# Adding the window mask on VectorE instead of on TensorE in six layers of local attention

## The reference

```python
mask = (it < jb) | (it > jb + w) | (jb == -1)
sim = jnp.einsum('bhwie,bhwje->bhwij', bq, bk2) * QK_SCALE
sim = jnp.where(mask, -jnp.finfo(sim.dtype).max, sim)
attn = jax.nn.softmax(sim, -1)
...
for i in range(DEPTH):
    x = attn_layer(shift_tokens(x), Wqkv[i], q_scale[i], k_scale[i], Wo[i]) + x
    x = ffn_layer(shift_tokens(x), ln_g[i], ln_b[i], W1[i], b1[i], W2[i], b2[i]) + x
```

## Time and profile before

| what | value |
|---|---|
| time, median of 3 runs | 3788.91 us (3785.52 to 3793.87) |
| time of the profiled execution | 3794.89 us |
| its span on the core | 3793.1 us |
| mean granted TensorE clock over the span | 0.936 |
| TensorE matmul busy | 3143.8 us (83%) |
| VectorE busy | 2479.8 us (65%) |
| ScalarE busy | 2071.4 us (55%) |
| GpSimd busy | 2292.4 us (60%) |

### The profile page before, as it was taken

The page is one execution under the profiler, slowest core; times in us unless marked ns, Lnnn a source line. Parts: engine busy times, 40 slices in busy tenths (PEclk is TensorE's granted clock), DMA queues, the critical chain, the costliest instruction groups (busy, mean ns, idle before and its releaser), DMA issues. The chain is left out here.

```text
span 3793.1 us, 121537 instructions
## 1 busy us (share of the span) xinstructions
PE 3143.8 (83%) x52983; PEld 2305.8 (61%) x52983; DVE 2479.8 (65%) x3404; ACT 2071.4 (55%) x2481; POOL 2292.4 (60%) x1606
## 2 busy tenths in 40 slices
PE   3169899899899998858888888888888888888885
PEld 2146677677677776636666666666666666666664
DVE  5456667677667776346676666766766766667664
ACT  2125555555555554426666666666666666666663
POOL 1334444444444543057777787777777777777773
PEclk7579999999999999979999999999999999999997
DMA  4344444445444444042222222322232222222221
GB/s 106 56 68 78 78 77 80 77 78 84 74 79 83 73 86 75 10 134 60 54 53 75 73 54 61 85 57 58 52 92 56 53 72 75 53 62 52 54 61 37
DMA packets 277483, 260.21 MB, mean 69 GB/s; under 512 B 106264, under 2 KB 220841, under 8 KB 276825
## 3 DMA queue, kind: packets, MB, share of 16 engines
q1 hardware_dynamic: 276232, 252.24, 31.3%
q10 hardware_dynamic: 720, 0.20, 0.0%
HBM read 98.30 MB, written 40.37 MB: 37 GB/s over the span
## 5 line engine op out<-in xcount | busy, mean ns | idle before, releaser
L659 ACT ACTIVATE prob<-psS 128x1024 f32<-128x1024 f32 x512 | 524.6, 1025 | 666.2 <-PE psS L536 664.5
L810 DVE TENSOR_TENSOR colmax<-psS,colmax 128x1024 f32<-128x1024 f32 x480 | 584.2, 1217 | 447.4 <-PE psS L536 447.2
L536 PE MATMUL psS<-diag,pst 128*128 128x64 bf16 x16384 | 596.2, 196 | 9.3 <-issue 9.3
L528 PE MATMUL psS<-qst,kst 48*128 48x128 bf16 (+1 forms) x8192 | 382.4, 224 | 257.6 <-DMA pst<-p_parts 187.1
L536 PEld LDWEIGHTS psS<-diag,pst 128*128 128x128 f16 x16384 | 530.3, 100 | 72.5 <-issue 21.2
L1263 PE MATMUL R<-wqkv,xsT 128*128 128x512 f32 x1152 | 557.5, 607 | 1.5 <-ACT qT L1399 1.1
L528 PEld LDWEIGHTS psS<-qst,kst 48*128 48x128 bf16 (+1 forms) x8192 | 241.6, 97 | 408.3 <-issue 157.3
L1527 POOL TENSOR_TENSOR pr<-pr,rnq 128x1024 f32<-128x1024 f32 x96 | 182.8, 1905 | 392.9 <-DVE pr L1608 392.9
L508 POOL TENSOR_TENSOR rel<-f,top 128x1024 f32<-128x1024 f32 x61 | 144.5, 2368 | 428.5 <-DVE top L815 428.0
L570 PE MATMUL psO<-prob,v 128*9 128x128 f32 x8192 | 329.3, 278 | 12.4 <-issue 11.8
L744 POOL TENSOR_TENSOR rel<-rel,rec 128x1024 f32<-128x1024 f32 x64 | 151.0, 2360 | 259.3 <-DVE rec L823 259.3
(11 more groups left out here) (190 smaller groups left out, 6274.5 us busy)
## 6 DMA issues: line engine op xcount, KB each, us to landing
v<-vs SPq DMA_DIRECT2D x576, 128.0 KB, 2.4
pst<-p_parts SPq DMA_DIRECT2D x512, 128.0 KB, 5.0
p_parts<-stage SPq DMA_DIRECT2D x64, 512.0 KB, 3.1
v<-vs SPq DMA_DIRECT2D x384, 64.0 KB, 2.0
wqkv<-in_L_ffn_Wqkv SPq DMA_DIRECT2D x18, 512.0 KB
q_stack<-qpart SPq DMA_DIRECT2D x6, 512.0 KB
qst<-q_stack SPq DMA_DIRECT2D x32, 96.0 KB, 6.0
wo<-in_L_ffn_Wo SPq DMA_DIRECT2D x6, 512.0 KB
```

The lines of the kernel that those rows point to most:

```text
L528: pe.matmul(dst[:, hp, P * p:P * (p + 1)], kst[r, pair, P * jb:P * (jb + 1)], qst[r, par, pair, :], start=(p == 0), stop=False, skip_group ...
L536: last = pe.matmul(o, pst[:, par, g, P * jb:P * (jb + 1)], diag[:, par, g, h0:h0 + HH // 2, :], start=False, stop=(g == NG - 1), skip_grou ...
L659: act.activation(prob[:, st % 2, :], psS[:, slot_of("b", st)].rearrange("p a b -> p (a b)"), ACT.Exp)\
L810: dve.tensor_tensor(dst, src, dst, ALU.max).then_inc(a_read, 1)
```

## The change

The mask is no longer put into R[3] by TensorE ahead of the scores. The score products open the accumulation themselves, and VectorE adds the float32 mask while it moves the scores from PSUM to `pr` in SBUF. The maximum and the subtraction then read `pr`. The output projection, which reuses R[3], waits for that addition (`masked_done`) and no longer for the subtraction. The bf16 copies of the mask and the identity, made once at the start, go away.

```diff
--- before.py
+++ after.py
@@ -1081,9 +1081,7 @@
         xm = sb("xm", [P, NB + 1, D])
         rope = sb("rope", [P, NB, 4 * LD])
         mask32 = sb("mask32", [P, 2, 2 * WIN])
-        mask = sb("mask", [P, NB, 2 * WIN], BF16)
         ident = sb("ident2", [P, P])
-        identb = sb("identb", [P, P], BF16)
         xs_a = sb("xs_a", [P, 2, D])
         xs_f = sb("xs_f", [P, D])
         xsT = sb("xsT", [P, 2, P])
@@ -1127,7 +1125,7 @@
 
         names = """init_dma init_dve init_pool w_dma xs_f_dma xT_done xT_ready q_done k_done v_done sq_done
             tq_done tk_done ssq_done clamp_done rn_done add_done kn_done qT_done kT_done qT_ready kT_ready
-            s_done mx_done sub_done scaled_done exp_done sum_done rden_done pT_done pT_ready pv2_done o_ready
+            s_done masked_done mx_done sub_done scaled_done exp_done sum_done rden_done pT_done pT_ready pv2_done o_ready
             oT_done oT_ready wo_done x2_done st_done lnv_done eps_done rstd_done xn_done xnT_done xnT_ready h_done
             hb_done gelu_done g_done gT_done gT_ready w2_done xmb_done x3_done v_ready tab_done prev_done q_added out_dma
             pool_taken dve_taken sp_taken""".split()
@@ -1216,9 +1214,6 @@
                 dve.memset(xm[:, 0, :], 0.0)
                 dve.memset(has_prev[:, 0:1], 0.0)
                 dve.memset(has_prev[:, 1:NB], 1.0)
-                dve.tensor_copy(identb[:], ident[:])
-                dve.tensor_copy(mask[:, 0, :], mask32[:, 0, :])
-                dve.tensor_copy(mask[:, 1:NB, :], mask32[:, 1:2, :].broadcast_to([P, NB - 1, 2 * WIN]))
                 dve.wait_ge(m["init_pool"], 6)
                 dve.tensor_tensor(xa[:, 1:NB + 1, :], xm[:, 1:NB + 1, :], mv16[:, :, 0:1].broadcast_to([P, NB, D]),
                                   ALU.subtract).then_inc(m["init_dve"], 1)
@@ -1343,16 +1338,12 @@
                         wait(pe, m["qT_ready"], n + 1)
                         wait(pe, m["kT_ready"], n + 1)
                         wait(pe, m["o_ready"], n)
-                        mk = slot(mask, n % NB)
-                        for half in range(2):
-                            pe.matmul(R[3][:, half, :], identb[:], mk.unsqueeze(1).broadcast_to([P, PAIRS, 2 * WIN]),
-                                      start=True, stop=False, skip_group_check=True)
                         for i in range(PAIRS):
                             for w in range(NW):
                                 last = pe.matmul(flat[3][WIN * w:WIN * (w + 1), P * i:P * (i + 1)],
                                                  qT[:, 1 - par, i, WIN * w:WIN * (w + 1)],
                                                  kT[:, 1 - par, i, :, WIN * w:WIN * (w + 2)],
-                                                 start=False, stop=True, skip_group_check=True)
+                                                 start=True, stop=True, skip_group_check=True)
                         last.then_inc(m["s_done"], 1)
                     if a:
 
@@ -1384,7 +1375,7 @@
 
                         wait(pe, m["oT_ready"], u + 1)
                         if b:
-                            wait(pe, m["sub_done"], n + 1)
+                            wait(pe, m["masked_done"], n + 1)
                         w = slot(wo, wp(u))
                         for i in range(PAIRS):
                             last = pe.matmul(flat[3][:, 0:D], otT[:, i, :], w[:, D * i:D * (i + 1)],
@@ -1601,13 +1592,15 @@
                         dve.tensor_tensor(gs[:], hs[:, 0, :], hs[:, 1, :], ALU.mult).then_inc(m["g_done"], 1)
                     if b:
                         wait(dve, m["s_done"], n + 1)
-                        dve.tensor_reduce(mx[:], flat[3].rearrange("p (h k) -> p h k", k=2 * WIN), AX.X, ALU.max)\
-                           .then_inc(m["mx_done"], 1)
+                        wait(dve, m["pT_done"], n)
+                        heads = pr[:].rearrange("p i a k -> p (i a) k")
+                        allowed = mask32[:, 0 if n % NB == 0 else 1, :].unsqueeze(1).broadcast_to([P, LH, 2 * WIN])
+                        dve.tensor_tensor(heads, flat[3].rearrange("p (h k) -> p h k", k=2 * WIN), allowed, ALU.add)\
+                           .then_inc(m["masked_done"], 1)
+                        wait(dve, m["masked_done"], n + 1)
+                        dve.tensor_reduce(mx[:], heads, AX.X, ALU.max).then_inc(m["mx_done"], 1)
                         wait(dve, m["mx_done"], n + 1)
-                        wait(dve, m["pT_done"], n)
-                        dve.tensor_tensor(pr[:].rearrange("p i a k -> p (i a) k"),
-                                          flat[3].rearrange("p (h k) -> p h k", k=2 * WIN),
-                                          mx[:].unsqueeze(2).broadcast_to([P, LH, 2 * WIN]), ALU.subtract)\
+                        dve.tensor_tensor(heads, heads, mx[:].unsqueeze(2).broadcast_to([P, LH, 2 * WIN]), ALU.subtract)\
                            .then_inc(m["sub_done"], 1)
                     if a:
                         rotate(s, par, 1, 1, "tk_done")
```

## The result

| | before | after |
|---|---|---|
| median | 3791.39 us (4 runs, 3785.52 to 3800.72) | 3993.07 us (4 runs, 3981.21 to 3996.27) |
| ratio, 95% interval | | 1.0523 [1.0505, 1.0542] |
| span of the profiled execution | 3793.1 us | 3979.4 us |
| mean granted TensorE clock over the span | 0.936 | 0.918 |

The account below looks back on a forecast made before the run. The prediction took a loop through GpSimd, TensorE, ScalarE and VectorE as the bound. 93 full steps times (23.9 - 21.75) give 200 us, with +3 and -3 at the edges; 3789 + 200 = 3989 us, range 3900 to 4010.

Parts of the forecast that it names:

- The bound: A loop through GpSimd, TensorE, ScalarE and VectorE sets the step, 21.13 us at full clock; VectorE's idle 2.86 us cannot help.
- The pass: VectorE's added pass between gate product and k rotation lies wholly on the loop: 1.24 us per step, bounds 1.16 to 1.30.
- Mask products: Removing them saves TensorE 0.59 us per step, but gate product and Gelu wait hide it: gain on the loop 0.
- release of R[3]: Output projection waits for the addition, but waited for the later copy of the attention output before: 0.
- initial copies: Removing the copies made once at the start, ahead of a wait for GpSimd, gives 0.
- The clock: TensorE's clock falls at the hidden layer and q transposes in nearly every step, making steps 23.9 us instead of 22.37.
- The mean clock: Sign: granted TensorE clock from first to last maximum goes down from 0.97 to about 0.93.
- TensorE's pause ahead of the q projection: Sign: TensorE stands still for about 1.3 us there, as the q projection waits for L1621, shifted by 1.24 us.
- GpSimd's idle time ahead of its scaling: Sign: GpSimd's wait ahead of L1527 grows by 1.2 us per unit.
- The rival of a second fall: A second clock fall per step behind the new pause slows the q projection: at worst 1.4 us per step, 4100 us; chance 0.05.
- Faster after all: Rival: TensorE's own list sets the end, so 43 to 56 us are gained, 3740 us; chance 0.02.
- two terms of 3 us: Units at both ends add 3 us; some steps after the start and around weight loads escape the fall, minus 3 us.

Follow-up runs that it names:

- the pass over 6 heads: Kernel before with one more VectorE pass, the mask again in SBUF over 6 of the 16 heads, behind the subtraction: 3884.56 us, ratio 1.0248.
- the filler: Two TensorE products per step with unused results, in the quiet stretch ahead of the hidden layer: kernel after 3846.73 us, kernel before 3731.13 us.
- two passes: Kernel after with the mask added a second time, in SBUF, by one more VectorE pass between addition and maximum: 3988.02 us, ratio 1.0522.

## Why the prediction was right

*The bound.* The loop through GpSimd, TensorE, ScalarE and VectorE was read rightly: work on it costs in full (22.40 - 21.14 = 1.26 us for the pass), work beside it costs nothing (mask products away: 0).

*The pass.* Forecast 1.24 us, measured 1.25 at full clock (22.38 - 21.13). The passes took 1.22, 1.22 and 1.23 us. The maximum was no cheaper from SBUF (1.220 mean), the subtraction no cheaper with both operands there (1.225). GpSimd stood idle throughout, 6.16 us in the step shown, so nothing could contend. The Trainium skill's rule on the shared SBUF interfaces (GPSIMD Engine Reference, Key points) was thus not put to the test by any run here.

*Mask products, release of R[3], initial copies.* Forecast 0. The first was tested alone (0), the two others were seen only in the trace: the output projection still starts behind the copy of the attention output, not behind VectorE.

*The clock.* Forecast: nearly every step a long one of 23.9 us; measured: 91 of 95 within 23.87 to 24.04. This term, 86 of the 202 us, came from the argument that a long step fits the distance of the falls and can adjust to it. The 24.0 us in it was carried on from two distances between three falls, and that it came out was in part luck. The traces bear it out afterwards. Before, 23 of 36 distances between falls are 64.9 us and 10 are 44.4; with the pass over 6 heads 25 of 55 are 44.4 and 21 are 23.9; after, 90 of 94 are 23.9. The same distances come back while the step at full clock goes from 21.13 to 22.38 us. The after-trace also shows the adjusting: steps that began at 24.04 and 23.97 settle at 23.89 within a few, and after a disturbance (23.94, then 23.87) they do so again. What disturbed them is not shown; the one at 2614 us does not lie at a weight load, as these start at 2467 and 2849 us.

That the falls are what costs there, and not a companion of something else, is shown by the filler. That the number of long steps does not simply grow with the step is shown by four lengths at full clock: 21.1 us gives 33 of 87, 21.7 us 50, 22.4 us all, 23.6 us ten. But in the last of these the pause ahead of the q projection is wider too, and most of its falls moved there, so it doesn't show what the length alone would do: that step and falls fall into time with each other is the reading that fits all traces, and not one that a run singles out. What makes the falls keep their distance of 23.9 us is not shown by any run.

The Trainium skill, TensorE: Matmul & The Clock Gate, section on how the gate oscillates in real kernels, tells of a loop that pauses and is throttled again each round: this trace now does so in 94 of 95 rounds, nearly as that section has it, though TensorE does not stand still in its pause (1.31 us busy of 3.40); the kernel before, with the same pause, did so in three of eight.

*Signs named ahead.* The mean clock fell from 0.97 to 0.93 as forecast, and TensorE's pause ahead of the q projection came to 1.42 us against about 1.3 (its own terms, 1.24 + 0.3 to 0.5 - 0.16, give 1.4 to 1.6). GpSimd's idle time ahead of its scaling was to grow by 1.2 us per unit and grew by 2.1 (201.6 / 96): it bears the falls as well as the pass, which the forecast of that sign forgot.

*The rival of a second fall* was ruled out for this change rightly (each step has one). Its price of at most 1.4 us per step was too high: with two passes, where the q projection did run at half clock, most steps paid nothing. Its total was added up wrongly too, as 3989 + 93 x 1.4 is 4119 us and not 4100.

*Faster after all*, by 43 to 56 us: the run without the products shows 0.

The sum: 93 x (23.89 - 21.76) = 198 of the 200 us forecast. Of the two terms of 3 us that cancelled, the second was wrong in its reason: only the first step escaped the fall, and none did around the weight loads. The profiled span came to 3979.4, 14 us under the forecast 3993, while the three other runs of the kernel lie at 3992 to 3996. Some 11 us of this lie ahead of the first gate product, which came at 1707.2 us against 1717.9 in the trace before. It lies anywhere between 1702.9 and 1724.4 in the eleven traces, so the work ahead of it varies from run to run by more than the terms of 3 us.

## What to carry to other kernels

Find the loop through the engines before counting busy shares: on it 1.2 us cost 1.2 us per round, while two products on the busiest engine were free; and an idle stretch of an engine only takes work that is issued ahead of what it waits for. Where TensorE has a quiet stretch in each round, compare the granted clock of single rounds, long against short: a small lengthening can turn an occasional fall into one per round, and two unused products in idle time bought back 1.6% before the change and 3.7% after it. When a step is held at such a length, a measured "costs nothing" is no licence: the second pass was free only because the first had already paid for it.

## What was not expected of the hardware

That a kernel with twice the added VectorE work runs in the same time (3988 and 3993 us) was expected, but for another reason. The falls of the clock did not become rare. Most moved from L1325 and L1334, on the loop, to the q projection, beside it: 3.63 us instead of 1.95 and a step of 23.63 us all the same. And they kept their 23.9 us from one to the next although the step was shorter than that.
